# Two-branch graph convolution: shorter first turns, splits in three pieces, block additions held behind the split

## The chip, the cores and the metric

One core of one Trainium2 chip runs the whole program. The metric is the device time of one execution in microseconds; the median of the runs is compared, and a profile of one execution is at hand.

## What is computed

```python
def _gcn_layer(x, adj, W, b):
    d_inv_sqrt = (jnp.sum(adj, axis=1) + 1e-09) ** (-0.5)
    msg = d_inv_sqrt[:, None] * adj * d_inv_sqrt[None, :] @ x
    return jax.nn.relu(msg @ W + b)
H_f = _gcn_layer(feature_x, adj, W_f, b_f)
H_s = _gcn_layer(spatial_x, adj, W_s, b_s)
attn = jax.nn.sigmoid(jnp.concatenate([H_f, H_s], axis=1) @ W_att + b_att)
out = _layernorm(x + attn * H_f + (1.0 - attn) * H_s, axis=-1)
```

`adj` is 4096 x 4096 in f32, both feature matrices are 4096 x 128. The heavy part is `adj @ (d * [x, spatial_x])`, a 4096 x 4096 by 4096 x 256 product. The scale `d` of a row needs the sum over that whole row of `adj`.

## The kernel before

The contraction is cut into 32 j-tiles of 128 rows (t = 0 to 31) and the output columns into eight groups of 512 (g0 to g7). A block is one j-tile against one group; an **item** is four blocks, and there are 64 items. `plan` (L24) writes their order by hand. Blocks of one group that follow one another accumulate in PSUM as a **run**; four runs at a time form a **turn** of a set of groups, g0 to g3 or g4, g6, g5, g7, and the two sets alternate. The front (items 0 to 47) walks through j-tiles 0 to 23: the early turns take one, two or three tiles, the later ones four, where the two old tiles come first ("column" items, two tiles of two groups) and the two new tiles behind ("spread" items, one tile of four groups).

Each item passes through these queues:

- SyncE (SP) issues all loads in one fixed order: `load_item` (L333) brings the 1 MB `raw` block of item k into one of three buffers, `load_part` (L345) half a j-tile's rows of `adj` (`nat`, 1 MB) for the row sums, and `load_x` (L358) feature rows. `load_item(k)` waits until item k-3 was split and, where it was added up, until its block additions are done.
- ScalarE (ACT): `row_sum` (L696) of the parts listed under `parts[k]`, then `high` (L685), which rounds `raw` into `Ah`. After the first piece of an item it makes `Yh` of a new j-tile (`y_high`, L709), which waits for the scale `D`.
- GpSimd (POOL): for each k first `degree` (L796), which turns the two row sums of a tile into `D`, then `sum_block` (L834), which adds two of the four blocks of an item of the set g4 to g7 into `S` (these sums serve the last tiles' scales). The order on POOL is fixed: `degree`, `sum_block`, next k.
- VectorE (DVE): `low` (L489) makes `Al = raw - Ah`, `y_low` (L498) makes `Yl`, and `evacuate` (L517) moves finished runs from PSUM into `acc`.
- TensorE (PE): `block_of` (L390) issues six 128x512 matmuls per block (`Ah` with `Yh`, `Ah` with `Yl`, `Al` with `Yh`, for two halves), 24 per item. In a spread item a block's two halves follow each other, in a column item both tiles come in one half and then in the other (`sweeps`, L90).

`high` and `low` work in pieces (L305): item 0 in four, items 1 to 19 (`HALVED`) in two of 1024 columns, later items whole. For items below `HALVED` the order on DVE is: two runs of the turn that ended, first piece, `y_low`, one more run, second piece, last run (L616 to L635). A block on PE waits for the piece that holds it (L467).

The items of the front, with their j-tile (u: set g0 to g3, v: set g4 to g7, c: column item):

```
item   0   1   2   3   4   5   6   7   8   9   10    11    12  13  14    15    16  17
       0u  0v  1v  1u  2u  2v  3v  3u  4u  5u  45vc  45vc  6v  7v  67uc  67uc  8u  9u
```

Of the kernel before, what the change touches and what calls it, by code (L numbers as in the profile page):

```python
# [13 lines left out]
GT = 4  # L14
# [2 lines left out]
NATS = 3  # L17
YRING = 8
ROWS = 12
HALVED = 20  # L20
WARM = [14, 8, 3]


def plan(T):  # L24

    G = T // GT
    FRONT = T - 2 * GT
    runs, items = [], []

    def add_runs(gs, tiles, pairs):
        new = [len(runs) + i for i in range(len(gs))]  # L40
        runs.extend((g, tiles, pair, (0, IB)) for g, pair in zip(gs, pairs))
        return new

    def column(new, tiles):
        blocks = [(e, t) for e in new for t in tiles]
        items.extend(blocks[i:i + 4] for i in range(0, len(blocks), 4))

    def spread(new, tiles):
        items.extend([(e, t) for e in new] for t in tiles)

    sets = [[0, 1, 2, 3], [4, 6, 5, 7]]
    for n, tiles in enumerate([[0], [0, 1], [1, 2], [2, 3], [3, 4, 5]]):
        spread(add_runs(sets[n % 2], tiles, range(4)), tiles)
    for n in range(3, FRONT // 2):
        old, fresh = [2 * n - 2, 2 * n - 1], [2 * n, 2 * n + 1]
        new = add_runs(sets[n % 2], old + fresh, range(4))
        column(new, old)
        spread(new, fresh)
    tiles = [FRONT - 2, FRONT - 1]
    column(add_runs(sets[0], tiles, [0, 1, 2, 0]), tiles)  # L60

    first = len(runs)
    s6, s7 = list(range(FRONT, FRONT + GT)), list(range(FRONT + GT, T))
    runs.extend((g, s6 + s7, (g + 1) % 3, (0, IB)) for g in range(G - 1))
    runs.append((G - 1, s6 + s7, 2, (0, IB // 2)))
    runs.append((G - 1, s6 + s7, 0, (IB // 2, IB)))
    order = [(0, s6), (1, s6), (0, s7), (1, s7)] + [(g, s) for g in range(2, G - 1) for s in (s6, s7)]
    order += [(G - 1, s6 + s7), (G, s6 + s7)]
    items.extend([(first + g, t) for t in s] for g, s in order)
    return runs, items  # L70


def build(nc, At, adj, xs_in, W_f, W_s, b_f, b_s, W_att, b_att, out):
# [5 lines left out]
    G = T // GT  # L79
# [4 lines left out]
    FINAL = K - 2 * G  # L84
# [43 lines left out]
    PLAIN_FROM = len(SUMMED) * P  # L128
    parts = {k: [] for k in range(K)}
    parts[0], parts[2] = [0, 1], [2, 3]  # L130
    parts[4], parts[6], parts[8], parts[9] = [4, 5], [6, 7], [8, 9], [10, 11]
    for n in range(12, 30):
        parts[n - 2].append(n)
    for n in range(30, 2 * FULL):
        parts[n - 3].append(n)
# [27 lines left out]
    y_at = {k: [] for k in range(K)}  # L163
    for r in range(T):
        y_at[y_position(r)].append(r)
    X_AFTER = {y_position(m * GT) - (2 if m == 1 else 4): m for m in range(1, G)}
    assert len(X_AFTER) == G - 1

    H_F, H_S, H_ALL = slice(0, H), slice(H, H2), slice(0, H2)
    DIF = slice(H2, H2 + F)  # L170
# [26 lines left out]
    with ExitStack() as ctx:  # L197
# [6 lines left out]
        def sem(name):  # L204
            return ctx.enter_context(nc.semaphore(name))
# [40 lines left out]
        raw0_in = [sem("raw0_first"), sem("raw0_second")]  # L246
        nat1_first = sem("nat1_first")
        nat_in = [sem(f"nat_in{i}") for i in range(NATS)]
        x_early = [sem("x_first"), sem("x_second")]
        xs_sem = [sem(f"xs_in{i}") for i in range(G)]  # L250
        const_in = sem("const_in")
        pool_const = sem("pool_const")
        rs_act = sem("rs_act")
# [10 lines left out]
        low_ok = sem("low_ok")  # L264
# [40 lines left out]
        def pieces(k):  # L305

            if k == 0:
                return [(i, i + 1) for i in range(GT)]
            return [(0, 2), (2, GT)] if k < HALVED else [(0, GT)]

        def z_of(r):

# [20 lines left out]
        def _(sp):  # L333
# [24 lines left out]
            def load_x(m):  # L358
                sp.dma_start(xs[:, m * GT:(m + 1) * GT, :], xs_v[m]).then_inc(xs_sem[m], 16)

            sp.dma_start(xs[:, 0:1, :], xs_v[0, :, 0:1, :]).then_inc(x_early[0], 16)
            for k in range(K):
                for n in parts[k]:
                    load_part(n)
                if k == 2:
                    sp.dma_start(xs[:, 1:2, :], xs_v[0, :, 1:2, :]).then_inc(x_early[1], 16)
                if k == 4:
                    sp.dma_start(xs[:, 2:GT, :], xs_v[0, :, 2:GT, :]).then_inc(xs_sem[0], 16)
                load_item(k)
                if k in X_AFTER:  # L370
                    load_x(X_AFTER[k])
                if k == FINAL + 1:
                    sp.dma_start(Wfs[:, 0:H], W_f).then_inc(const_in, 16)
                    sp.dma_start(Wfs[:, H:H2], W_s).then_inc(const_in, 16)
                    sp.dma_start(bias[:, 0:H], bf_v).then_inc(const_in, 16)
                    sp.dma_start(bias[:, H:H2], bs_v).then_inc(const_in, 16)
                    sp.dma_start(watt[:, :], watt_v).then_inc(const_in, 16)
                    sp.dma_start(batt[:, :], batt_v).then_inc(const_in, 16)
# [109 lines left out]
        def _(dve):  # L488
# [124 lines left out]
            for k in range(K):  # L613
                ended = [e for e in evac_order if end_item[e] == k - 2]
                ending = [e for e in evac_order if end_item[e] == k - 1]
                if k < HALVED:  # L616
                    evacuate_new(ending[:2])
                else:
                    if len(ended) == GT:
                        evacuate_new(ended[:3])  # L620
                    if len(ending) == GT:
                        evacuate_new(ending[:1])
                for a, b in pieces(k):
                    low(k, a, b)
                    if a == 0:
                        if k >= HALVED and len(ending) == GT:
                            evacuate_new(ending[:2])
                        if k in (FINAL - 1, FINAL):
                            evacuate_new(ending[:1])
                        for r in y_at[k]:  # L630
                            y_low(r)
                        if k < HALVED:
                            evacuate_new(ending[:3])
                if k < HALVED or k in (FINAL - 1, FINAL):
                    evacuate_new(ending)  # L635
                if k == COLLECT + 2:
                    column_sums()
                mixing, joining = group_at(k, L_MIX), group_at(k, L_JOIN)
                if mixing is not None:
                    for r in of_group(mixing):  # L640
                        affine(r)
                if joining is not None:
                    for r in of_group(joining):
                        join(r)
                if mixing is not None:
                    for r in of_group(mixing):
                        logit(r)
                if k < K - 1:
                    evacuate_new(ended)
# [34 lines left out]
        def _(act):  # L684
# [23 lines left out]

            def y_high(r):  # L709
                act.wait_ge(D_ok, r + 1)  # L710
                if r < 2:
                    act.wait_ge(x_early[r], 16)
                else:
                    act.wait_ge(xs_sem[r // GT], 16)
                if r >= YRING:
# [79 lines left out]
        def _(pool):  # L795
# [36 lines left out]
                pool.tensor_tensor(D[:, a:b], dg[:, a:b], mhalf[:, 0:b - a], ALU.pow).then_inc(D_ok, b - a)  # L832

            def sum_block(k, j):  # L834
                g = runs[items[k][j][0]][0] - BY_COLUMN[0]
                n = blocks_summed(k - 1) + summed_blocks(k).index(j)
                raw_here(pool, k)
                if n >= 1:
                    pool.wait_ge(block_sum_ok, n)
                pool.tensor_tensor(S[:, g, :], S[:, g, :], raw[:, k % RAWS, j * IB:(j + 1) * IB],  # L840
# [96 lines left out]
```

## Time and profile before

| | us |
|---|---|
| median of 3 runs | 394.38 (394.3 to 394.52) |
| the profiled execution, its own time | 394.35 |
| its span, first to last instruction | 392.6 |
| PE busy in the span | 376.2 |
| DVE, ACT, POOL busy | 303.9, 283.8, 161.8 |

The span is 1.75 us shorter than the execution. Times in the rows further down are counted from the start of the span. A busy PE says only that some matmul is in its pipeline: how fast it goes is seen from the starts of consecutive matmuls.

### The profile page before, as it was taken

How to read it: one execution, taken by the hardware profiler on the slowest of the kernel's cores; microseconds unless marked ns; L12 is line 12 of the kernel's file. 1: busy time of each engine (PE TensorE's matmuls, PEld its weight loads, DVE VectorE, ACT ScalarE, POOL GpSimd, SP SyncE). 2: the span in 40 equal slices, each digit the busy share in tenths (PEclk: the TensorE clock that was granted, in tenths of full speed). 3: DMA queues.
4: the chain of work that ended last, by engine and by line, in shares of the span. 5: the costliest groups of instructions: out<-in, count | busy, mean ns of one | idle time of the engine just before them, and what ended most of it. 6: DMA issues, size and time to landing. Idle time of an engine off the chain costs nothing. (4 is left out here: it accounts for less than half of the span.)

```text
span 392.6 us, 5474 instructions
## 1 busy us (share of the span) xinstructions
PE 376.2 (96%) x1778; PEld 314.7 (80%) x1778; DVE 303.9 (77%) x434; ACT 283.8 (72%) x364; POOL 161.8 (41%) x199
## 2 busy tenths in 40 slices
PE   7779999999999999999999999999999999999990
PEld 7668778778888888888888888888788888888990
DVE  2889996979668875959589593929977887888896
ACT  3777788788878887887868887878633566668464
POOL 2343601770067603782259200010000427787764
PEclk9999999999999999999999999999999999999996
DMA  7999999999999999999999999999575434354001
GB/s 276 424 416 423 419 419 424 418 422 419 422 417 422 425 417 423 417 422 422 419 422 419 414 416 421 417 416 390 222 276 191 192 124 187 126 194 122 28 28 54
DMA packets 24508, 130.77 MB, mean 333 GB/s; under 512 B 2848, under 2 KB 7840, under 8 KB 10400
## 3 DMA queue, kind: packets, MB, share of 16 engines
q1 hardware_dynamic: 24480, 130.43, 82.6%
q8 instruction: 14, 0.23, 0.2%
q14 instruction: 14, 0.11, 0.1%
HBM read 128.32 MB, written 2.10 MB: 332 GB/s over the span
## 5 line engine op out<-in xcount | busy, mean ns | idle before, releaser
L398 PE MATMUL sums<-Ah,Yh 128*128 128x512 f32 (+1 forms) x528 | 203.7, 386 | 5.4 <-DVE Yl L503 5.0
L400 PE MATMUL sums<-Al,Yh 128*128 128x512 f32 (+1 forms) x528 | 202.1, 383 | 0.0
L399 PE MATMUL sums<-Ah,Yl 128*128 128x512 f32 (+1 forms) x528 | 202.1, 383 | 0.0
L494 DVE TENSOR_TENSOR Al<-raw,Ah 128x2048 fp32r<-128x2048 f32 (+2 forms) x86 | 159.5, 1861 | 32.2 <-ACT Ah L690 32.2
L690 ACT ACTIVATE Ah<-raw 128x2048 fp32r<-128x2048 f32 (+2 forms) x86 | 125.8, 1475 | 50.4 <-DMA raw<-in_At 31.5
L398 PEld LDWEIGHTS sums<-Ah,Yh 128*128 128x128 f32 x528 | 99.2, 188 | 27.3 <-DVE Yl L503 6.6
L400 PEld LDWEIGHTS sums<-Al,Yh 128*128 128x128 f32 x528 | 99.2, 188 | 19.6
L399 PEld LDWEIGHTS sums<-Ah,Yl 128*128 128x128 f32 x528 | 99.3, 188 | 19.0
L700 ACT ACTIVATE nat<-nat 128x2048 f32<-128x2048 f32 (+1 forms) x54 | 100.1, 1854 | 19.8 <-DMA nat<-in_adj 19.1
L514 DVE TENSOR_TENSOR acc<-sums,acc 128x512 f32<-128x512 f32 (+1 forms) x122 | 78.3, 675 | 36.6 <-PE sums L400 36.6
L840 POOL TENSOR_TENSOR S<-S,raw 128x512 f32<-128x512 f32 x40 | 69.2, 1730 | 27.5 <-DMA raw<-in_At 24.3
L798 POOL TENSOR_SCALAR dg<-rs 128x1 f32<-128x1 f32 x23 | 15.5, 672 | 106.4 <-ACT nat L700 106.2
L846 POOL TENSOR_TENSOR fin<-fin 128x128 f32<-128x128 f32 x29 | 13.9, 478 | 33.5 <-ACT fin L724 33.5
L733 ACT ACTIVATE fin<-xs,less 128x128 f32<-128x128 f32 x30 | 11.7, 390 | 17.9 <-POOL less L852 17.9
L503 DVE SCALAR_TENSOR_TENSOR Yl<-xs,D,Yh 128x256 fp32r<-128x256 f32 x32 | 22.0, 702 | 0.0
L847 POOL TENSOR_TENSOR xs<-xs,fin 128x128 f32<-128x128 f32 x29 | 20.7, 713 | 0.0
L558 DVE SCALAR_TENSOR_TENSOR xs<-fin,att,xs 128x128 f32<-128x128 f32 x30 | 12.3, 423 | 8.6 <-POOL xs L847 8.5
L717 ACT ACTIVATE Yh<-xs,D 128x256 fp32r<-128x256 f32 x32 | 15.4, 496 | 3.5 <-PE sums L400 1.8
L801 POOL TENSOR_TENSOR D<-dg,mhalf 128x1 f32<-128x1 f32 x23 | 15.8, 689 | 1.9
L408 PEld LDWEIGHTS sums<-Wfs,acc 128*128 128x128 f32 x128 | 15.6, 191 | 0.7
L408 PE MATMUL sums<-Wfs,acc 128*128 128x128 f32 x128 | 16.0, 276 | 0.0
L724 ACT ACTIVATE fin<-nat 128x256 f32<-128x256 f32 x32 | 11.4, 408 | 4.8 <-DVE nat L528 4.7
(51 smaller groups left out, 135.7 us busy)
## 6 DMA issues: line engine op xcount, KB each, us to landing
raw<-in_At SPq DMA_DIRECT2D x63, 1024.0 KB, 9.0
nat<-in_adj SPq DMA_DIRECT2D x47, 1024.0 KB, 11.6
nat<-in_adj SPq DMA_DIRECT2D x8, 768.0 KB, 9.4
xs<-in_xs SPq DMA_DIRECT2D x7, 512.0 KB, 10.4
out<-xs SPq DMA_DIRECT2D x32, 64.0 KB, 1.6
nat<-in_adj SPq DMA_DIRECT2D x2, 512.0 KB, 6.9
raw<-in_At SPq DMA_DIRECT2D x2, 512.0 KB, 8.3
xs<-in_xs SPq DMA_DIRECT2D x2, 128.0 KB, 7.0
```

The source lines that it names most:

```text
L398: pe.matmul(to, Yh[:, t % YRING, hs], high, start=first, stop=False)
L399: pe.matmul(to, Yl[:, t % YRING, hs], high, start=False, stop=False)
L400: mm = pe.matmul(to, Yh[:, t % YRING, hs], low, start=False, stop=last)
L408: return pe.matmul(sums[:, 3, bank, c + half * H:c + (half + 1) * H], acc[:, r // GT, half, q * P:(q + 1) * P], Wfs[:, half * H:(half + 1) ...
L494: dve.tensor_tensor(Al[:, k % SPLITS, a * IB:b * IB], raw[:, k % RAWS, a * IB:b * IB], Ah[:, k % SPLITS, a * IB:b * IB], ALU.subtract).the ...
L503: dve.scalar_tensor_tensor(out=Yl[:, r % YRING, :], in0=xs[:, r, :], scalar=D[:, r:r + 1], in1=Yh[:, r % YRING, :].bitcast(F32), op0=ALU.mult,
L514: dve.tensor_tensor(acc[:, g, half, a:b], sums[:, pair, half, 0:b - a], acc[:, g, half, a:b], ALU.add).then_inc(evac_ok, 1)
L690: act.activation(Ah[:, k % SPLITS, a * IB:b * IB], raw[:, k % RAWS, a * IB:b * IB], ACT.Copy).then_inc(high_ok, b - a)
L700: act.activation(nat[:, n % NATS, 0:width], nat[:, n % NATS, 0:width], ACT.Copy, accum_out=rs[:, r, h:h + 1]).then_inc(rs_act, 1)
L801: pool.tensor_tensor(D[:, r:r + 1], dg[:, r:r + 1], mhalf[:, 0:1], ALU.pow).then_inc(D_ok, 1)
L840: pool.tensor_tensor(S[:, g, :], S[:, g, :], raw[:, k % RAWS, j * IB:(j + 1) * IB], ALU.add).then_inc(block_sum_ok, 1)
L847: pool.tensor_tensor(xs[:, r, 0:F], xs[:, r, 0:F], f[:, H_S], ALU.add).then_inc(res_ok, 1)
```

## The change

The first turns are now of tiles 0; 0, 1; 1, 2; 2, 3; 3, 4; 4, 5; and 5, 6, 7, so there is one turn more, and every later turn goes to the other set. The early items up to 19 are split in three pieces (one block, one block, two blocks) on ACT and DVE, with `y_low` behind the first piece and the third run's evacuation behind the second. `sum_block` waits until all four blocks of its item are split. Five parts of the row sums (10 to 14) are due one item later, and the features of tiles 2 to 11 arrive two tiles at a time, in front of the item at which they are due; the first feature row is loaded behind the first parts.

```diff
-HALVED = 20
+STEPWISE = 20
...
-    for n, tiles in enumerate([[0], [0, 1], [1, 2], [2, 3], [3, 4, 5]]):
+    for n, tiles in enumerate([[0], [0, 1], [1, 2], [2, 3], [3, 4], [4, 5], [5, 6, 7]]):
         spread(add_runs(sets[n % 2], tiles, range(4)), tiles)
-    for n in range(3, FRONT // 2):
+    for n in range(4, FRONT // 2):
         old, fresh = [2 * n - 2, 2 * n - 1], [2 * n, 2 * n + 1]
-        new = add_runs(sets[n % 2], old + fresh, range(4))
+        new = add_runs(sets[(n + 1) % 2], old + fresh, range(4))
...
-    column(add_runs(sets[0], tiles, [0, 1, 2, 0]), tiles)
+    column(add_runs(sets[1], tiles, [0, 1, 2, 0]), tiles)
...
-    parts[4], parts[6], parts[8], parts[9] = [4, 5], [6, 7], [8, 9], [10, 11]
-    for n in range(12, 30):
+    parts[4], parts[6], parts[8], parts[10] = [4, 5], [6, 7], [8, 9], [10, 11]
+    parts[11], parts[12], parts[13] = [12], [13], [14, 15]
+    for n in range(16, 30):
         parts[n - 2].append(n)
...
-    X_AFTER = {y_position(m * GT) - (2 if m == 1 else 4): m for m in range(1, G)}
+    X_EARLY = [(0, 1), (1, 2), (2, 4), (4, 6), (6, 8), (8, 10), (10, 12)]
+    X_BEFORE = {y_position(a): i for i, (a, b) in enumerate(X_EARLY) if i >= 1}
+    X_AFTER = {y_position(m * GT) - 4: m for m in range(3, G)}
...
-            return [(0, 2), (2, GT)] if k < HALVED else [(0, GT)]
+            return [(0, 1), (1, 2), (2, GT)] if k < STEPWISE else [(0, GT)]
...
-            sp.dma_start(xs[:, 0:1, :], xs_v[0, :, 0:1, :]).then_inc(x_early[0], 16)
             for k in range(K):
                 for n in parts[k]:
                     load_part(n)
-                if k == 2:
-                    sp.dma_start(xs[:, 1:2, :], xs_v[0, :, 1:2, :]).then_inc(x_early[1], 16)
-                if k == 4:
-                    sp.dma_start(xs[:, 2:GT, :], xs_v[0, :, 2:GT, :]).then_inc(xs_sem[0], 16)
+                if k == 0:
+                    load_x_early(0)
+                if k in X_BEFORE:
+                    load_x_early(X_BEFORE[k])
                 load_item(k)
...
                         for r in y_at[k]:
                             y_low(r)
-                        if k < HALVED:
-                            evacuate_new(ending[:3])
+                    elif a == 1:
+                        evacuate_new(ending[:3])
...
                 raw_here(pool, k)
+                pool.wait_ge(low_ok, GT * (k + 1))
                 if n >= 1:
                     pool.wait_ge(block_sum_ok, n)
```

The items of the front are now:

```
item   0   1   2   3   4   5   6   7   8   9   10  11  12  13  14    15    16  17
       0u  0v  1v  1u  2u  2v  3v  3u  4u  4v  5v  5u  6u  7u  67vc  67vc  8v  9v
```

Two places of the new order matter below. The first is POOL, from the additions of item 5 on (`S`: block additions, `dg` and `D`: the two steps of `degree`, here for tiles 3, 4 and 5). Before:

```order
L840 TENSOR_TENSOR S<-S,raw 128x512 [waits block_sum_ok,raw_in2] x2
L798 TENSOR_SCALAR dg<-rs 128x1 [waits rs_act]
L801 TENSOR_TENSOR D<-dg,mhalf 128x1 [waits dg_ok]
L840 TENSOR_TENSOR S<-S,raw 128x512 [waits block_sum_ok,raw_in0] x2
L798 TENSOR_SCALAR dg<-rs 128x1 [waits rs_act]
L801 TENSOR_TENSOR D<-dg,mhalf 128x1 [waits dg_ok]
L798 TENSOR_SCALAR dg<-rs 128x1 [waits rs_act]
L801 TENSOR_TENSOR D<-dg,mhalf 128x1 [waits dg_ok]
```

Now, for the same tiles, with the additions of items 5, 6 and 9:

```order
L849 TENSOR_TENSOR S<-S,raw 128x512 [waits block_sum_ok,low_ok,raw_in2] x2
L805 TENSOR_SCALAR dg<-rs 128x1 [waits rs_act]
L808 TENSOR_TENSOR D<-dg,mhalf 128x1 [waits dg_ok]
L849 TENSOR_TENSOR S<-S,raw 128x512 [waits block_sum_ok,low_ok,raw_in0] x2
L805 TENSOR_SCALAR dg<-rs 128x1 [waits rs_act]
L808 TENSOR_TENSOR D<-dg,mhalf 128x1 [waits dg_ok]
L849 TENSOR_TENSOR S<-S,raw 128x512 [waits block_sum_ok,low_ok,raw_in0] x2
L805 TENSOR_SCALAR dg<-rs 128x1 [waits rs_act]
L808 TENSOR_TENSOR D<-dg,mhalf 128x1 [waits dg_ok]
```

The additions wait for `low_ok` as well, and those of item 9 now stand in front of tile 5's `degree`; those of item 5 stood in front of tile 3's already, without that wait.

The second place is DVE at items 14 and 15 (column items; `Yl` is that of tile 8, which item 16 is the first to use). Before:

```order
L514 TENSOR_TENSOR acc<-sums,acc 128x512 [waits evac_ok,half_done] x4
L494 TENSOR_TENSOR Al<-raw,Ah 128x1024 [waits raw_in2,high_ok,early_done]
L514 TENSOR_TENSOR acc<-sums,acc 128x512 [waits evac_ok,half_done] x2
L494 TENSOR_TENSOR Al<-raw,Ah 128x1024 [waits raw_in2,high_ok,early_done]
L514 TENSOR_TENSOR acc<-sums,acc 128x512 [waits evac_ok,half_done] x2
L494 TENSOR_TENSOR Al<-raw,Ah 128x1024 [waits raw_in0,high_ok,early_done]
L503 SCALAR_TENSOR_TENSOR Yl<-xs,D,Yh 128x256 [waits early_done,D_ok,Yh_ok]
L494 TENSOR_TENSOR Al<-raw,Ah 128x1024 [waits raw_in0,high_ok,early_done]
```

Now:

```order
L521 TENSOR_TENSOR acc<-sums,acc 128x512 [waits evac_ok,half_done] x4
L501 TENSOR_TENSOR Al<-raw,Ah 128x512 [waits high_ok,raw_in2,early_done] x2
L521 TENSOR_TENSOR acc<-sums,acc 128x512 [waits evac_ok,half_done] x2
L501 TENSOR_TENSOR Al<-raw,Ah 128x1024 [waits raw_in2,high_ok,early_done]
L521 TENSOR_TENSOR acc<-sums,acc 128x512 [waits evac_ok,half_done] x2
L501 TENSOR_TENSOR Al<-raw,Ah 128x512 [waits high_ok,raw_in0,early_done]
L510 SCALAR_TENSOR_TENSOR Yl<-xs,D,Yh 128x256 [waits early_done,D_ok,Yh_ok]
L501 TENSOR_TENSOR Al<-raw,Ah 128x512 [waits high_ok,raw_in0,early_done]
L501 TENSOR_TENSOR Al<-raw,Ah 128x1024 [waits raw_in0,high_ok,early_done]
```

In item 15 (`raw_in0`) only one block now stands in front of `Yl`, where two stood, and the turn at items 14 to 17 is now of the set that is added up on POOL.

## Rows read from the trace of the kernel before

**Rows 1.** The page, busy us of each engine, share of the span, instructions.
```profile
PE 376.2 (96%) x1778; PEld 314.7 (80%) x1778; DVE 303.9 (77%) x434; ACT 283.8 (72%) x364; POOL 161.8 (41%) x199
```
**Rows 2.** Busy time by stretch (from:to, us, engines, clock, DMA share, GB/s).
```profile
100.00:280.00 180.00, 180.00 (x804) 149.29 (x803) 131.51 (x125) 143.39 (x133) 68.20 (x60) 1.00 1.00 412
```
**Rows 3.** Waits of the whole span: total us, times, longest.
```profile
POOL dg L798 <- ACT nat L700: 106.2, 21, 10.3
...
PE sums L398 <- DVE Yl L503: 5.0, 3, 2.2
...
PEld sums L398 <- DVE Al L494: 1.4, 3, 0.6
```
**Rows 4.** Timeline of PE (start, took), 88 matmuls in step, first and last.
```profile
120.06 0.39 PE L399 MATMUL sums<-Ah,Yl 128*128 128x512 f32 x1
...
139.78 0.39 PE L399 MATMUL sums<-Ah,Yl 128*128 128x512 f32 x1
```
**Rows 5.** Timeline of PE around the first matmuls of items 2, 6, 10, 13.
```profile
23.73 0.39 PE L400 MATMUL sums<-Al,Yh 128*128 128x512 f32 x1
26.30 0.50 PE L398 MATMUL sums<-Ah,Yh 128*128 128x512 f32 x1 [2.18 <-DVE Yl L503]
26.63 0.40 PE L399 MATMUL sums<-Ah,Yl 128*128 128x512 f32 x1
...
48.25 0.39 PE L400 MATMUL sums<-Al,Yh 128*128 128x512 f32 x1
49.42 0.50 PE L398 MATMUL sums<-Ah,Yh 128*128 128x512 f32 x1 [0.78 <-DVE Yl L503]
...
71.14 0.39 PE L400 MATMUL sums<-Al,Yh 128*128 128x512 f32 x1
71.67 0.50 PE L398 MATMUL sums<-Ah,Yh 128*128 128x512 f32 x1
...
87.90 0.39 PE L400 MATMUL sums<-Al,Yh 128*128 128x512 f32 x1
88.41 0.50 PE L398 MATMUL sums<-Ah,Yh 128*128 128x512 f32 x1
```
**Rows 6.** Timeline of DVE: copies, splits of two widths, Yl alone and beside POOL.
```profile
12.45 1.90 DVE L494 TENSOR_TENSOR Al<-raw,Ah 128x512 fp32r<-128x512 f32 x3
14.26 2.48 DVE L511 COPY acc<-sums 128x512 f32<-128x512 f32 x4
...
36.61 0.48 DVE L503 SCALAR_TENSOR_TENSOR Yl<-xs,D,Yh 128x256 fp32r<-128x256 f32 x1
...
41.63 1.21 DVE L494 TENSOR_TENSOR Al<-raw,Ah 128x1024 fp32r<-128x1024 f32 x1
...
47.87 1.50 DVE L503 SCALAR_TENSOR_TENSOR Yl<-xs,D,Yh 128x256 fp32r<-128x256 f32 x1
```
**Rows 7.** Timeline of POOL: degree, and additions in pairs.
```profile
14.47 2.73 POOL L840 TENSOR_TENSOR S<-S,raw 128x512 f32<-128x512 f32 x2 [3.18 <-DMA raw<-in_At]
...
43.75 0.30 POOL L798 TENSOR_SCALAR dg<-rs 128x1 f32<-128x1 f32 x1 [3.27 <-ACT nat L700]
44.13 1.46 POOL L801 TENSOR_TENSOR D<-dg,mhalf 128x1 f32<-128x1 f32 x1
45.57 3.52 POOL L840 TENSOR_TENSOR S<-S,raw 128x512 f32<-128x512 f32 x2
...
55.35 0.56 POOL L801 TENSOR_TENSOR D<-dg,mhalf 128x1 f32<-128x1 f32 x1
```
**Rows 8.** Timeline of ACT: rounding of one and two blocks, Yh.
```profile
11.73 1.66 ACT L690 ACTIVATE Ah<-raw 128x512 fp32r<-128x512 f32 x3
...
22.32 1.06 ACT L690 ACTIVATE Ah<-raw 128x1024 fp32r<-128x1024 f32 x1 [0.87 <-DMA raw<-in_At]
...
45.63 0.51 ACT L717 ACTIVATE Yh<-xs,D 128x256 fp32r<-128x256 f32 x1 [0.36 <-POOL D L801]
```
**Rows 9.** The page, DMA issues: line, count, KB each, median us to landing.
```profile
raw<-in_At SPq DMA_DIRECT2D x63, 1024.0 KB, 9.0
```

More of the change, by code:

```diff
@@ L165, in build @@
         y_at[y_position(r)].append(r)
-    X_AFTER = {y_position(m * GT) - (2 if m == 1 else 4): m for m in range(1, G)}
-    assert len(X_AFTER) == G - 1
+    X_EARLY = [(0, 1), (1, 2), (2, 4), (4, 6), (6, 8), (8, 10), (10, 12)]
+    X_BEFORE = {y_position(a): i for i, (a, b) in enumerate(X_EARLY) if i >= 1}
+    X_AFTER = {y_position(m * GT) - 4: m for m in range(3, G)}
+    assert len(X_BEFORE) == len(X_EARLY) - 1 and len(X_AFTER) == G - 3
     H_F, H_S, H_ALL = slice(0, H), slice(H, H2), slice(0, H2)
@@ L248, in build @@
         nat_in = [sem(f"nat_in{i}") for i in range(NATS)]
-        x_early = [sem("x_first"), sem("x_second")]
-        xs_sem = [sem(f"xs_in{i}") for i in range(G)]
+        x_early = [sem(f"x_early{a}") for a, b in X_EARLY]
+        xs_sem = {m: sem(f"xs_in{m}") for m in range(3, G)}
         const_in = sem("const_in")
@@ L359, in load_x, with load_x_early @@
                 sp.dma_start(xs[:, m * GT:(m + 1) * GT, :], xs_v[m]).then_inc(xs_sem[m], 16)
-            sp.dma_start(xs[:, 0:1, :], xs_v[0, :, 0:1, :]).then_inc(x_early[0], 16)
+            def load_x_early(i):
+                a, b = X_EARLY[i]
+                c = a % GT
+                sp.dma_start(xs[:, a:b, :], xs_v[a // GT, :, c:c + b - a, :]).then_inc(x_early[i], 16)
             for k in range(K):
@@ L615, in _ @@
                 ending = [e for e in evac_order if end_item[e] == k - 1]
-                if k < HALVED:
+                if k < STEPWISE:
                     evacuate_new(ending[:2])
@@ L625, in _ @@
                     if a == 0:
-                        if k >= HALVED and len(ending) == GT:
+                        if k >= STEPWISE and len(ending) == GT:
                             evacuate_new(ending[:2])
@@ L631, in _ @@
                             y_low(r)
-                        if k < HALVED:
-                            evacuate_new(ending[:3])
-                if k < HALVED or k in (FINAL - 1, FINAL):
+                    elif a == 1:
+                        evacuate_new(ending[:3])
+                if k < STEPWISE or k in (FINAL - 1, FINAL):
                     evacuate_new(ending)
@@ L710, in y_high @@
                 act.wait_ge(D_ok, r + 1)
-                if r < 2:
-                    act.wait_ge(x_early[r], 16)
+                if r < X_EARLY[-1][1]:
+                    act.wait_ge(next(x_early[i] for i, (a, b) in enumerate(X_EARLY) if r < b), 16)
                 else:
```

## The prediction

> **What bounds it now.** I read the busy times first: PE has 376.2 of 392.6 us [rows 1]. The stretches show where that holds: from 100 to 280 us PE is busy without a gap at full granted clock, and DMA is full as well [rows 2]. PE's own pace stands in its timeline: 87 steps take 19.72 us, so a matmul starts every 0.2267 us and an item of 24 lasts 5.44 us [rows 4]. Nothing beside PE matters there unless it makes PE wait. The view of waits says where that happens: PE waits three times, 5.0 us together, for `Yl`, the low half of a new j-tile's features, and the weight loads three times for the split `Al`, 0.6 us at most [rows 3]. In the timeline these are the first matmuls of items 2, 6, 10 and 13 [rows 5]. A stall is the step from the matmul in front less 0.2267, plus 0.11, because the second step after a wait is 0.33 instead of 0.2267. That gives 2.45 us (item 2), 1.05 (6), 0.41 (10) and 0.39 (13). For items 1 and 5, which wait for the split, I take 0.5 together, an estimate from the row with 1.4 us in three waits. The sum is **4.8 us**, all ahead of 90 us: that is all the change can win in the stream. The reader should also see that POOL's `degree` waited 106.2 us in 21 waits for row sums [rows 3], so the scale `D` is made the moment its row sum is there. POOL is never late for it.
>
> **The prices.** Copies and evacuations start every 0.60 us: (2.48 - 0.68) / 3, where 0.68 is one copy [rows 6]. A 512-wide split takes 0.69 and the next starts after 0.605, (1.90 - 0.69) / 2 [rows 6]; a 1024-wide one takes 1.21 [rows 6]. Two additions on POOL take 2.73 us alone and 3.52 with a two-input DVE instruction between them [rows 7]. `dg` is 0.30, `D` 0.56 [rows 7]; with about 0.08 between, a `degree` is 0.94. From `D` to the first matmul: `Yh` 0.51 [rows 8], `Yl` 0.48 [rows 6], and 0.2 for three hand-overs, estimated at under 0.1 each from the one shown, `D` ending at 44.13 + 1.46 = 45.59 and `Yh` starting at 45.63 [rows 7, 8]: 1.19.
>
> **The step that decides: `degree` queued behind additions that now start late.** Take a turn's first item k of the set that POOL adds up (items 5 and 9, followed by a new tile). Count from the start of item k-1. The second run of the old turn leaves PE after twelve matmuls, at 2.94 (12 x 0.2267, 0.16 for the last to drain, 0.06 hand-over). DVE then does its last copy (0.60), two one-block splits (1.21), two evacuations (1.2) and the two-block split (1.21): 7.16, which is 1.72 after item k begins. Before, the additions ran when `raw` had landed; now they start here. They take 2.73 to 3.52; I take 3.1, because the next item's first split falls between them. Then `degree`, 0.94, and 1.19 to PE: 1.72 + 0.06 + 3.1 + 0.94 + 1.19 = 7.0. PE wants the tile at 5.44. The stall is 1.5, with the restart **1.6 us at item 6 and 1.6 at item 10**; by the ends 2.73 and 3.52 it is 1.3 to 2.1. Queued behind the late `D` are POOL's next additions, on ACT the rest of `high` (it stands behind `y_high`), on DVE the rest of the split, and on SP the load of item k+3.
>
> **Item 2.** Copies from 14.26 [rows 6], then the same chain: 14.26 + 2.4 + 1.21 + 1.2 + 1.21 = 20.3. Additions until 23.1. Item 2's first split (its `raw` is rounded from 22.32 [rows 8]) gets in front of `dg`, which I take as 0.4 lost: `D` is there at 23.1 + 0.4 + 0.94 = 24.4 and PE starts at 25.6. It could start at 23.6 (23.73 + 0.23 [rows 5], less 0.3 for item 1's wait, which goes). With the restart **2.2 us**. Here the one-block piece and the undisturbed `Yl` win back what the late `degree` loses. **Items 1 and 5**: the split is in time, 0. **Item 13**: its two row sums now both stand in item 13 on ACT; I leave its 0.4 as it was, between 0 and 0.8.
>
> **Item 15.** POOL's turn is now at items 14 to 17. Item 14's split ends 1.7 to 2.6 after it begins (2.6 if DVE comes late out of item 13's stall). Tile 8's `degree` is behind item 14's additions, `D` at 5.5 to 6.6. Item 15 does not need tile 8, but its second block stands behind `y_high` on ACT and `y_low` on DVE. From `D`: 0.04, 0.40 until `Yh` lets the next go, 0.63 rounding a block ((1.66 - 0.63) / 2 = 0.52 apart [rows 8]), 0.1, 0.67 split and hand-over: 1.84, so 7.3 to 8.4. As a column item it wants its second block three matmuls in, at 6.12. Stall 1.2 to 2.3, restart 0.1: I take **2.1**, nearer the upper end, because DVE does come late. Before, two blocks stood in front of `Yl` and there were no additions here.
>
> **Item 17** needs tile 9, whose `degree` is behind the additions of items 15 and 16, two pairs in a row of 2.73 to 3.52 each from the end of item 15's split, against two items of 5.44: 0 to 1.9, I take **1.2**. **Small ones**: the third piece arrives 0.2 to 0.3 late at items 3, 7, 11 and 18, where DVE started late, with the restart about 0.35 each; and at items 24 to 26 ACT, held by `y_high` of tile 12, is up to 1.2 late. That is 0 to 2.6; I take half, **1.3**.
>
> **Costed at nothing.** Four more runs are eight evacuations, 4.8 us of DVE, and the third piece adds 0.076 to each of 19 items: both lie beside PE, except as counted above. The Trainium skill, VectorE: DVE Perf Modes, section on the TRN2 errata (SBUF-src ops pay a fixed extra latency per instruction), puts an instruction at (N + 151) / 0.96 ns, so a further piece would cost 0.157 us. The durations here agree, 0.69 for 512; the starts, 0.605 apart, do not, since instructions overlap. By the page the stalls at items 6 and 10 would each be 0.08 longer. The first feature row moves behind three loads: `nat` goes out one issue earlier, but the start hangs on `raw` landing, rounding and split, so 0. Feature pairs let the `raw` behind them land earlier, which nobody waits for. Loads of items k+3 leave some 3 us later; 9.0 us lie between issue and landing in the median [rows 9], so 6 stay.
>
> **Sum.** After: 2.2 + 1.6 + 1.6 + 0.4 + 2.1 + 1.2 + 1.3 = 10.4. Before: 4.8. The difference is +5.6 on the profiled execution's 394.35, which stands 0.03 under the median of the runs: **400.0 us**. With all low ends (2.2, 1.3, 1.3, 0, 1.3, 0, 0) it is 6.1 and 395.7; with all high ends (2.2, 2.1, 2.1, 0.8, 2.4, 1.9, 2.6) 14.1 and 403.7.
>
> **Rivals.**
> - *Faster.* `Yl` took 1.50 beside an addition and 0.48 alone [rows 6]: DVE and POOL hold each other up. Additions behind the split fall beside evacuations, which go unhurt: four copies in 2.48 from 14.26 [rows 6] while POOL added from 14.47 [rows 7]. If `D` is in time, items 6, 10 and 13 lose nothing, and item 2 only 0.7 (22.32 + 0.63 + 1.2 = 24.15): 4.8 becomes 1.1, **390.7 us**. It decides if the last piece ends by 0.5 after item k begins (5.44 less 2.73, 0.94, 1.19), which would need DVE 1.2 us earlier; against it stands the run that PE frees only at 2.94. The Trainium skill, GPSIMD Engine Reference, Specifications, says the same of the port: contention comes with DVE instructions with two SBUF inputs. The trace agrees, and by that rule alone this would be the result. Chance 0.10.
> - *The late turn is harmless.* If DVE has worked ahead at items 14 to 17, only items 2, 6, 10 and 13 stall: 5.8, so 395.4; with item 6 and 10 at their low ends it is within the noise. Chance 0.15, a third of it within 0.2%.
> - *Loads starve.* If the 3 us later issue leaves DMA idle, about 1 us at four of the held loads, landings slip by 4: **404 us**. For it: DMA is full [rows 2]; against it: rows 9. Chance 0.09.
>
> **Numbers.** The forecast has 0.66, the rivals 0.15, 0.09 and 0.10. Range 395.2 to 404.0: the two ends of the sum and most of the second and third rival. 0.2%, 0.8 us, is about what a measurement of this kernel can tell from no change. Faster 0.10, same 0.05, slower 0.85.
>
> **What would show it.** In the changed profile: POOL's `dg` is released by its own queue instead of ACT, its wait for `nat` falls well under 106 us; additions in pairs of 2.73 beside evacuations; `Yl` at 0.48; PE waits for `Yl` of about 1.5 at items 6 and 10, and for `Al` inside item 15. I am wrong if `dg` still follows its row sum at once, or if PE runs through items 9 to 18 without a wait over 0.5 us.

## The result, and the profile after

The changed kernel takes **408.53 us** in the median of 5 runs (407.39 to 409.42), the kernel before 394.52 in 5 runs beside it (394.3 to 394.64): a ratio of 1.0358, 95% interval 1.0337 to 1.0379, so +14.0 us, slower. The forecast had the side and the mechanism, but less than half of the size: 400.0, with 404.0 as the upper end. The profiled execution took 409.42 (span 407.6), 15.07 over that of before. Where an execution of a kernel below was disturbed, its time is left out; for two kernels (wait late only; first feature row first, wait kept) that was the profiled one, so they are told by times alone.

The page of the changed kernel; the first line answers to [rows 1], the second is the granted TensorE clock in 40 slices, the group lines have busy us and mean ns of one, then the idle time before and what ended most of it; the last answers to [rows 9].

```profile
PE 381.8 (94%) x1778; PEld 314.9 (77%) x1778; DVE 301.6 (74%) x461; ACT 280.5 (69%) x383; POOL 146.4 (36%) x199
...
PEclk9699999999999999999999999999999999999996
...
L849 POOL TENSOR_TENSOR S<-S,raw 128x512 f32<-128x512 f32 x40 | 58.8, 1470 | 101.9 <-issue 71.6
L724 ACT ACTIVATE Yh<-xs,D 128x256 fp32r<-128x256 f32 x32 | 15.5, 500 | 47.1 <-POOL D L808 47.1
L805 POOL TENSOR_SCALAR dg<-rs 128x1 f32<-128x1 f32 x23 | 13.1, 567 | 65.5 <-ACT nat L707 64.5
...
raw<-in_At SPq DMA_DIRECT2D x63, 1024.0 KB, 7.8
```

DVE and POOL are *less* busy than before, though DVE has 27 instructions more: what they were meant to win, they won. An addition takes 1.47 us in the mean, and the feature operations are quick. But additions wait 71.6 us for something that isn't a transfer, and ACT waits 47.1 us for `D`, in 15 of 32 tiles.

The view of waits of the changed kernel (total us, times, longest), beside [rows 3]:

```profile
POOL S L849 <- issue: 71.6, 11, 11.1
POOL dg L805 <- ACT nat L707: 64.5, 13, 8.4
ACT Yh L724 <- POOL D L808: 47.1, 15, 7.4
...
POOL S L849 <- DVE Al L501: 26.9, 6, 12.3
...
PE sums L405 <- DVE Yl L510: 9.7, 6, 3.2
```

`dg` follows its row sum in 13 cases instead of 21, and that wait fell from 106.2 to 64.5: in the others `degree` stood behind additions. PE now waits 9.7 us for `Yl`, 5.0 before.

PE's timeline at items 6, 10, 15 and 17, which the forecast named, then at items 24, 25 and 35, which it did not (what stands in brackets is the idle time in front); the first group answers to [rows 5].

```profile
50.50 0.39 PE L407 MATMUL sums<-Al,Yh 128*128 128x512 f32 x1
52.27 0.50 PE L405 MATMUL sums<-Ah,Yh 128*128 128x512 f32 x1 [1.38 <-DVE Yl L510]
...
76.25 0.50 PE L405 MATMUL sums<-Ah,Yh 128*128 128x512 f32 x1 [1.38 <-DVE Yl L510]
...
106.47 0.50 PE L405 MATMUL sums<-Ah,Yh 128*128 128x512 f32 x1 [1.52 <-DVE Al L501]
...
118.00 0.50 PE L405 MATMUL sums<-Ah,Yh 128*128 128x512 f32 x1 [0.99 <-DVE Yl L510]
...
157.51 0.47 PE L405 MATMUL sums<-Ah,Yh 128*128 128x512 f32 x1 [0.63 <-DVE Al L501]
...
164.82 0.50 PE L405 MATMUL sums<-Ah,Yh 128*128 128x512 f32 x1 [1.61 <-DVE Yl L510]
...
221.35 0.50 PE L405 MATMUL sums<-Ah,Yh 128*128 128x512 f32 x1 [1.30 <-DVE Al L501]
```

By the forecast's own measure (the step less 0.2267, and the slower second step) items 2 to 18 lose 9.5 us, items from 20 on 6.9; before it was 4.8 and about 0.4. The start costs the rest. PE's first matmul in the kernel before, then the first ones in the changed kernel, and its clock from 13.2 to 16.2 us (from:to, us, engines' busy time, clock, DMA share, GB/s):

```profile
12.55 0.50 PE L398 MATMUL sums<-Ah,Yh 128*128 128x512 f32 x1 [2.03 <-DVE Yl L503]
...
13.27 0.80 PE L405 MATMUL sums<-Ah,Yh 128*128 128x512 f32 x1 [3.25 <-DVE Yl L510]
13.86 0.63 PE L406 MATMUL sums<-Ah,Yl 128*128 128x512 f32 x1
...
19.28 0.40 PE L407 MATMUL sums<-Al,Yh 128*128 128x512 f32 x1
```

```profile
13.20:16.20 3.00, 2.93 (x7) 2.35 (x8) 2.44 (x5) 1.85 (x5) 0.00 (x0) 0.50 1.02 431
```

PE was idle for 3.25 us, and then the granted clock is 0.50, that is 1.2 GHz: 14 steps take 6.01 us instead of 3.17. Before, the first matmul stood at 12.55 behind 2.03 us of idling, and the clock was 1.00 (2.4 GHz) from 12.5 to 16 us. With the start at 13.27 instead of 12.55 that is 2.73 (2.84 less the slower second step, which both have) + 0.72 = 3.45. **The ledger of the profiled executions**: 3.45 + (9.5 - 4.8) + (6.9 - 0.4) = 14.65 of 15.07. Of the 6.9, 5.3 lie in items 24 to 41; 1.6 lie at the end of the front (PE's steps at 292.65 and 296.10).

### The profile page after: what moved, and what is told of

The parts are those of the page before. It is cut to its first block and busy times, and to the rows that moved or that the text cites. A ratio compares the mean times of both kernels' runs of the same rounds, so it can differ in the third digit from the quotient of the medians.

```text
span 407.6 us, 5537 instructions
## 1 busy us (share of the span) xinstructions
PE 381.8 (94%) x1778; PEld 314.9 (77%) x1778; DVE 301.6 (74%) x461; ACT 280.5 (69%) x383; POOL 146.4 (36%) x199
## 5 line engine op out<-in xcount | busy, mean ns | idle before, releaser
L405 PE MATMUL sums<-Ah,Yh 128*128 128x512 f32 (+1 forms) x528 | 206.4, 391 | 14.8 <-DVE Yl L510 9.7
L501 DVE TENSOR_TENSOR Al<-raw,Ah 128x2048 fp32r<-128x2048 f32 (+2 forms) x105 | 157.0, 1507 | 41.9 <-ACT Ah L697 41.0
L521 DVE TENSOR_TENSOR acc<-sums,acc 128x512 f32<-128x512 f32 (+1 forms) x130 | 82.9, 675 | 19.0 <-PE sums L407 19.0
L849 POOL TENSOR_TENSOR S<-S,raw 128x512 f32<-128x512 f32 x40 | 58.8, 1470 | 101.9 <-issue 71.6
L724 ACT ACTIVATE Yh<-xs,D 128x256 fp32r<-128x256 f32 x32 | 15.5, 500 | 47.1 <-POOL D L808 47.1
L805 POOL TENSOR_SCALAR dg<-rs 128x1 f32<-128x1 f32 x23 | 13.1, 567 | 65.5 <-ACT nat L707 64.5
L510 DVE SCALAR_TENSOR_TENSOR Yl<-xs,D,Yh 128x256 fp32r<-128x256 f32 x32 | 16.5, 532 | 24.0 <-ACT Yh L724 24.0
L855 POOL TENSOR_TENSOR fin<-fin 128x128 f32<-128x128 f32 x29 | 13.9, 479 | 31.5 <-ACT fin L731 31.5
L415 PE MATMUL sums<-Wfs,acc 128*128 128x128 f32 x128 | 16.2, 277 | 0.1
L808 POOL TENSOR_TENSOR D<-dg,mhalf 128x1 f32<-128x1 f32 x23 | 12.9, 561 | 1.9
```

The lines of the kernel that those rows point to most:

```text
L405: pe.matmul(to, Yh[:, t % YRING, hs], high, start=first, stop=False)
L415: return pe.matmul(sums[:, 3, bank, c + half * H:c + (half + 1) * H], acc[:, r // GT, half, q * P:(q + 1) * P], Wfs[:, half * H:(half + 1) ...
L501: dve.tensor_tensor(Al[:, k % SPLITS, a * IB:b * IB], raw[:, k % RAWS, a * IB:b * IB], Ah[:, k % SPLITS, a * IB:b * IB], ALU.subtract).the ...
L510: dve.scalar_tensor_tensor(out=Yl[:, r % YRING, :], in0=xs[:, r, :], scalar=D[:, r:r + 1], in1=Yh[:, r % YRING, :].bitcast(F32), op0=ALU.mult,
L521: dve.tensor_tensor(acc[:, g, half, a:b], sums[:, pair, half, 0:b - a], acc[:, g, half, a:b], ALU.add).then_inc(evac_ok, 1)
L724: act.activation(Yh[:, r % YRING, :], xs[:, r, :], ACT.Copy, scale=D[:, r:r + 1]).then_inc(Yh_ok, 1)
```

## The experiments

Theory 1 was the forecast's: `degree` queues on POOL behind additions that now wait for the split. The rivals: the loads (their order at the start, or loads held by late additions), and the third piece. Each ratio is to the kernel before on the same chip, with its 95% interval.

**The one line, taken out and put in alone.** First the changed kernel without it; then the kernel before with it and nothing else.

```diff
                 raw_here(pool, k)
-                pool.wait_ge(low_ok, GT * (k + 1))
                 if n >= 1:
```

> The changed kernel without the one added wait: block additions start when their raw block has landed, all else as changed. Theory 1 (the additions, held back, hold degree and so D, Yh, Yl): the waits of PE for Yl and for the split inside items fall from about 14 us to 5 or less, additions run beside the splits again (pairs of 3.5 us), 397 to 399.5 us, of which some 3 us are the slow start. Rival (one turn more, the third piece and the other set make DVE late by themselves): less than half of the loss goes, 403 us or more.

> The kernel before with that one wait added and nothing else. Theory 1: the larger part of the loss appears with this line alone, 401 to 406 us, with POOL waiting for the split and ACT for D. Rival (turns, pieces and set): 396 us or less. The start is untouched in both: first matmul at 12.55 us.

Measured: 393.98 us without the line (0.9989, 0.9979 to 0.9998), and 410.63 with the line alone (1.0406, 1.0389 to 1.0424). The line is the whole loss; all the rest of the change together is worth 0.4 us (0.1 to 0.8 by the interval). Both went further than theory 1 expected (397 to 399.5, and 401 to 406): in particular the slow start, for which it had kept 3 us, costs nothing without the line. Without it, the waits read as before:

```profile
POOL dg L805 <- ACT nat L707: 116.6, 21, 11.3
...
POOL S L848 <- DMA raw<-in_At: 23.4, 9, 4.5
...
PE sums L405 <- DVE Yl L510: 4.6, 4, 2.8
```

**The order of the first loads.** The changed kernel with the first feature row at the head again, then the kernel before with it behind the first parts.

```diff
+            load_x_early(0)
             for k in range(K):
                 for n in parts[k]:
                     load_part(n)
-                if k == 0:
-                    load_x_early(0)
```

> The changed kernel with the first feature row loaded ahead of the first parts again. Theory 2 (the order of the first loads makes the first block land 0.7 us later and the wait before the first matmul longer, which the clock answers with its lower level for some 6 us): first matmul at 12.55, matmuls in steps of 0.227 from there, 404.5 to 406 us. Rival (the start differs from run to run, whatever the order): no change, 407.4 to 409.4.

> The kernel before with the first feature row loaded behind the first parts, nothing else. Theory 2: the first block lands near 11.4 instead of 10.6, first matmul near 13.3, the lower clock level after it, 396.5 to 398.5 us, with runs that scatter by 2 us. Rival: 394.5, no scatter.

Measured: 407.04 to 408.39 (1.0331, 1.0314 to 1.0349), about 1 us under the changed kernel, with intervals that overlap; and 394.52 (1.0001, 0.9992 to 1.001). So theory 2, that the order of the first loads costs time, falls for the kernel before. The trace of that kernel with the order turned shows why: the start was late and slow there as well, and item 2 took it up.

```profile
12.87 0.50 PE L399 MATMUL sums<-Ah,Yh 128*128 128x512 f32 x1 [2.80 <-DVE Yl L504]
...
13.87 0.63 PE L399 MATMUL sums<-Ah,Yh 128*128 128x512 f32 x1
...
26.58 0.50 PE L399 MATMUL sums<-Ah,Yh 128*128 128x512 f32 x1 [0.90 <-DVE Yl L504]
```

Item 2 waits 0.90 instead of 2.18 [rows 5] and starts 0.28 later than before. There `D` hangs on a row sum, not on PE. With the wait it hangs on the split, the split stands behind DVE's copies of item 0, and those follow PE: in the changed kernel the four copies start 1.28 apart (14.95 to 18.79), as three matmuls take 3 x 0.427. So there a slow start should go through to item 2. The kernel with the wait early only, the next experiment, bears this out: it is the same program up to item 19, its first 14 steps took 4.92 us instead of 6.01, and item 2 started at 27.45 instead of 28.30.

**The wait in one half of the items.**

```diff
-                pool.wait_ge(low_ok, GT * (k + 1))
+                if k < STEPWISE:
+                    pool.wait_ge(low_ok, GT * (k + 1))
```

> The changed kernel with the wait only in items 1 to 19, whose split goes in pieces of 512 and 1024. Theory 1 (the forecast's stalls of items 2 to 18 are right in size and what it missed lies behind item 20, each part on its own): 394.0 of the kernel without the wait, plus about 9.5 of stalls less the 2.5 that it has there, so 400 to 402. Rival (late stalls are the echo of early ones, which leave VectorE behind): this part alone gives 405 or more.

> The changed kernel with the wait only from item 20 on, whose split is one instruction of 2048. Theory 1 (what the forecast missed lies here, on its own): 394.0 plus the 6.5 of stalls that the changed kernel has behind item 20, so 399.5 to 402. Rival (late stalls are the echo of early ones): 396 or less.

Measured: early only 400.48 to 402.11 (1.0167, 1.0145 to 1.0189); late only 400.90 to 401.16 (1.0165, 1.0148 to 1.0182). Over the kernel without the wait that is 1.0167 - 0.9989 and 1.0165 - 0.9989, 7.0 and 6.9 us; together 13.9, and the whole wait costs 1.0358 - 0.9989, 14.5. The halves add up: late stalls are no echo of early ones. The stretches agree. First the changed kernel, then the one with the wait early only:

```profile
120.00:200.00 80.00, 77.74 (x340) 63.19 (x339) 58.96 (x59) 61.36 (x58) 29.33 (x28) 1.00 1.00 407
200.00:280.00 80.00, 78.21 (x351) 64.12 (x350) 49.32 (x47) 58.21 (x54) 24.31 (x26) 1.00 0.95 388
```

```profile
120.00:200.00 80.00, 79.97 (x351) 65.44 (x351) 62.07 (x60) 66.00 (x60) 36.38 (x33) 1.00 1.01 420
200.00:280.00 80.00, 80.00 (x363) 66.26 (x362) 53.83 (x52) 63.42 (x60) 18.05 (x20) 1.00 1.01 418
```

Without the late wait PE is busy almost throughout, and DMA is full again.

**Degrees ahead of the additions.** The changed kernel with the wait, POOL's order turned (and the first feature row first); the same order in the kernel before with the wait; and the first again without the wait.

```diff
-            for k in range(1, FINAL):
+            for k in range(1, FINAL + 1):
                 for r in range(1, FULL):
-                    if last_part(r) in parts[k]:
+                    if k < FINAL and last_part(r) in parts[k]:
                         degree(r)
-                for j in summed_blocks(k):
-                    sum_block(k, j)
+                for j in summed_blocks(k - 1):
+                    sum_block(k - 1, j)
```

> The changed kernel, its wait kept, but on POOL each item's degrees go ahead of the additions of the item before (and the first feature row is loaded first again). Theory 1 (the loss is D made late, since degree queues behind additions that wait for the split): D follows its row sum again, POOL's wait of dg for nat is back near 100 us, and the time is 394 to 397. Rival (the loss is the loads held up by late additions, or additions that run beside the split): additions are as late or later than in the changed kernel, so the time stays at 402 or more.

> The kernel before with the wait added and, on POOL, degrees ahead of the additions of the item before. Theory 1 (degree queued behind late additions): nearly all of the 16.1 that the wait alone cost goes, 394 to 398. Rival (held loads, or additions beside the split): 403 or more.

> The changed kernel without the wait, degrees ahead of the additions of the item before, first feature row first. With the wait this order gave 398.5, 4 more than the kernel before. Theory (those 4 are the wait's: additions behind the split hold buffers and run beside other work): 393.5 to 395. Rival (they come from the order itself, since additions now wait for a row sum): 397 or more.

Measured: 398.48 (1.0104, 1.0085 to 1.0124), 399.5 (1.0129, 1.0106 to 1.0151) and 401.66 (1.0179, 1.0164 to 1.0193). Each of the first two lies between its theory and its rival: of +14 and +16 they leave +4 and +5. With the wait kept, and the additions about as late (those of item 5 begin 2.5 us after their item, those of item 6 1.8; in the changed kernel it is 1.8 and 2.4), 10 us came back, so additions that hold their buffers long are not the main cost. POOL's `dg` waits for row sums again. The second line is one of three late steps of PE at the end of the front:

```profile
POOL dg L804 <- ACT nat L706: 126.4, 22, 12.2
...
281.07 0.50 PE L404 MATMUL sums<-Ah,Yh 128*128 128x512 f32 x1 [0.97 <-DVE acc L520]
```

The third says that the order has a cost of its own, which theory 1 had not: without any wait it is 7 us slower than before, and 3 us slower than with the wait, so in this order the wait is a gain. Part of that is the clock: behind item 2's stall it was 0.50 from 26.3 to 29.3 us there, eight steps of about 0.43, some 1.6 us, and in the first kernel it was not. By the forecast's measure the first kernel loses 5.5 us from 22 to 270 us (the changed kernel 15.0, the kernel before 4.6, the third kernel 9.2) and 2.9 behind that (1.6, 0.3 and 3.1). So most of what it still loses lies at the end of the front, where the third kernel loses it without any wait. Why, I did not follow up, and since the order moves both parts, these three do not give the share of the queue in the loss.

**The wait only without, or only with, a degree behind.** Order, pieces and loads of the changed kernel. By this rule the first run has the wait in items 2, 6, 10, 15, 17, 23, 25, 30, 32 and 38 (item 33 has a degree behind it). The second run has the condition without its "not".

```diff
-                pool.wait_ge(low_ok, GT * (k + 1))
+                if not any(last_part(r) in parts[k + 1] for r in range(1, FULL)):
+                    pool.wait_ge(low_ok, GT * (k + 1))
```

> The changed kernel with the wait only at additions that have no degree directly behind them (items 2, 6, 10, 15, 17, 23, 25, 30, 32, 33 without one in the next item as the program counts them, and 38): order, pieces and loads as in the changed kernel. Theory (only a degree queued behind late additions costs): no loss, 392.5 to 394.8; and if additions beside evacuations spare VectorE, under 394.0 of the kernel without the wait. Rival (late additions as such cost, by the buffers and loads that they hold): half of the 14 stays, 398 or more.

> The changed kernel with the wait only at additions that have a degree directly behind them, in the next item (1, 5, 9, 14, 16, 22, 24, 31, 39 and the like). Theory (a degree queued behind late additions is the whole cost): as slow as the changed kernel, 405 to 410. Rival (late additions as such): about half of the loss, 399 to 403.

Measured: 397.07 to 398.09 (1.0083, 1.007 to 1.0096) without, 411.79 to 413.25 (1.0465, 1.045 to 1.048) with a degree behind. Waits with a degree right behind cost the whole loss and more. The others cost 3.7 (1.0083 - 0.9989), a quarter, between theory and rival. Most of what the second kernel loses beyond 408.5 is seen at item 15: its additions don't wait there, so they ran beside one-block splits, and two of these took 2.89 us together (1.28 is usual).

```profile
107.75 2.89 DVE L501 TENSOR_TENSOR Al<-raw,Ah 128x512 fp32r<-128x512 f32 x2
...
109.56 0.80 PE L405 MATMUL sums<-Ah,Yh 128*128 128x512 f32 x1 [2.84 <-DVE Al L501]
110.15 0.63 PE L406 MATMUL sums<-Ah,Yl 128*128 128x512 f32 x1
```

PE waited 2.84 instead of 1.52, and then ran at 1.2 GHz until 115.6 us (clock 0.50 from 109.5 to 115.5). In the first kernel items 6 and 10 no longer wait for `Yl`, and most of what is left lies behind item 20, where a late pair still delays a degree two items on:

```profile
180.42 1.30 POOL L850 TENSOR_TENSOR S<-S,raw 128x512 f32<-128x512 f32 x1 [4.63 <-issue]
181.89 6.11 POOL L850 TENSOR_TENSOR S<-S,raw 128x512 f32<-128x512 f32 x3 [0.17 <-POOL S L850]
188.09 2.22 POOL L805 TENSOR_SCALAR dg<-rs 128x1 f32<-128x1 f32 x1
```

These are the pairs of items 30 and 31, and the `dg` is item 32's. Only item 30's pair has a wait; item 31's came late because it stood behind it, and the degree behind both.

**The third piece.** With the wait, and without it (first feature row first; the second of the two has two pieces).

```diff
-            return [(0, 1), (1, 2), (2, GT)] if k < STEPWISE else [(0, GT)]
+            return [(0, 2), (2, GT)] if k < STEPWISE else [(0, GT)]
```

> The changed kernel, wait kept, with two pieces of two j-tiles in items 1 to 19 as before. Theory (the third piece costs what the forecast has as small stalls at items 3, 7, 11 and 18, 0.35 each): 1 to 1.5 faster than the changed kernel, 406.5 to 407.7. Rival (the piece of one j-tile lets PE start earlier behind each late feature tile, so it is a gain): 409 or more.

> The changed kernel without the wait and with the first feature row loaded first again. Theory (the slow start is taken up by the wait of item 2, as where the order of loads alone was changed): 393.7 to 394.2, as without the wait. Rival (here item 2 hardly waits, 0.6, so the start counts): 392.5 to 393.4.

> The changed kernel without the wait, first feature row first, two pieces. Theory (what is left of the change, short turns and the other set, is worth a few tenths, and the third piece nothing): within 0.4 of the same kernel with three pieces. Rival (the third piece holds up VectorE): 0.5 to 1.5 faster than it, the best kernel of the study.

Measured: 409.26 with the wait (1.0377, 1.0364 to 1.0391); without it 394.24 with three pieces (1.0000, 0.9991 to 1.0009) and 394.49 with two (1.0004, 0.9996 to 1.0013). The third piece loses nothing, and with the wait it may gain up to 1 us; the intervals overlap. The first feature row's place is worth nothing here either.

**A version with the wait only where it might help**: items 2, 6, 10, 15 and 17, and the same with the first feature row first.

```diff
-                pool.wait_ge(low_ok, GT * (k + 1))
+                if k < STEPWISE and not any(last_part(r) in parts[k + 1] for r in range(1, FULL)):
+                    pool.wait_ge(low_ok, GT * (k + 1))
```

> The changed kernel with the wait only in items 2, 6, 10, 15 and 17: before item 20 and with no degree directly behind. Theory (where nothing is queued behind, additions behind the split spare VectorE, as the missing stalls at items 6 and 8 of the last run suggest): 0.5 to 1.5 under the 394.0 of the kernel without the wait, 392.5 to 393.5. Rival (a wait never gains): 394 or more.

> The same, with the first feature row loaded first again. Theory (item 2 hardly waits here, so an earlier first matmul counts): 0.3 to 1 under the same kernel with the later load. Rival (item 2 takes it up): within 0.3 of it.

Measured: 394.63 (1.0007, 0.9999 to 1.0016) and 394.5 (1.0007, 0.9997 to 1.0017). No gain: the rival holds in both. The best kernel of the study is the changed one without its wait, 0.1% under the kernel before; with the first feature row first it measured the same as the kernel before (1.0000), so this is too little to be called a gain.

## Why the forecast had the side right and the size wrong

**The deciding step was right, to a tenth, at items 6 and 10.** The timeline of POOL, DVE and ACT around item 6 in the changed kernel, beside [rows 6 to 8]:

```profile
47.13 1.29 POOL L849 TENSOR_TENSOR S<-S,raw 128x512 f32<-128x512 f32 x1 [11.11 <-issue]
48.58 1.53 POOL L849 TENSOR_TENSOR S<-S,raw 128x512 f32<-128x512 f32 x1 [0.17 <-POOL S L849]
50.21 0.30 POOL L805 TENSOR_SCALAR dg<-rs 128x1 f32<-128x1 f32 x1
50.59 0.56 POOL L808 TENSOR_TENSOR D<-dg,mhalf 128x1 f32<-128x1 f32 x1
...
45.77 1.22 DVE L501 TENSOR_TENSOR Al<-raw,Ah 128x1024 fp32r<-128x1024 f32 x1
...
51.73 0.48 DVE L510 SCALAR_TENSOR_TENSOR Yl<-xs,D,Yh 128x256 fp32r<-128x256 f32 x1 [2.76 <-ACT Yh L724]
...
51.19 0.51 ACT L724 ACTIVATE Yh<-xs,D 128x256 fp32r<-128x256 f32 x1 [3.81 <-POOL D L808]
```

Item 5 begins at 50.50 + 0.23 - 5.44 = 45.29. Its split ends at 46.99, 1.70 later (forecast 1.72); the pair of additions takes 2.98 (3.1); `degree` ends at 51.15, 1.04 behind them (0.94); PE starts at 52.27, 1.12 after that (1.19). From item 5's start it is 6.98, and 7.0 was forecast.

**Item by item.** Items 6 and 10 lose 1.65 each (1.6), item 15 1.8 (2.1), item 17 1.3 (1.2), item 13 nothing (0.4), item 2 1.4 (2.2, for a start at 25.6; it starts at 28.30, after the slow start below, which delays PE as well as the chain). The third pieces of items 3, 7, 11 and 18 and the second steps there lose 1.7. Up to item 18 the sum is 9.5, where the forecast had 9.1 and 1.3 more for small ones. That the sums agree so closely is partly luck: items 2 and 13 lose 1.2 less than forecast, and the third pieces, of which the forecast had taken half, 1.7. (Two slips in the forecast's sums are small: 25.6 less 23.6 with the restart is 2.1 for item 2, not 2.2, and the rival *Faster* has 0.7 left, not 1.1, so 390.3.)

**The step that failed: "small ones", for the turns behind item 20.** The forecast had one turn there, at items 24 to 26, with ACT "up to 1.2 late", and took half. Items from 20 on measured 6.9 in the trace (6.5 over before), and 6.9 us in the run with the wait late only. Two things were not counted. POOL has a turn there three times (items 22 to 25, 30 to 33, 38 and 39), and the chain in it is longer, since rounding and split are one instruction of 2048 each. (The 1.6 us at the end of the front are not explained by this; PE waits 0.69 of them for a copy out of PSUM.) The timeline of POOL, DVE and ACT behind item 22's split in the changed kernel:

```profile
146.45 1.28 POOL L849 TENSOR_TENSOR S<-S,raw 128x512 f32<-128x512 f32 x1 [0.17 <-POOL S L849]
147.83 2.22 POOL L805 TENSOR_SCALAR dg<-rs 128x1 f32<-128x1 f32 x1
150.14 0.56 POOL L808 TENSOR_TENSOR D<-dg,mhalf 128x1 f32<-128x1 f32 x1
...
147.16 2.72 DVE L501 TENSOR_TENSOR Al<-raw,Ah 128x2048 fp32r<-128x2048 f32 x1
...
155.07 2.29 DVE L501 TENSOR_TENSOR Al<-raw,Ah 128x2048 fp32r<-128x2048 f32 x1 [1.64 <-ACT Ah L697]
...
150.73 0.51 ACT L724 ACTIVATE Yh<-xs,D 128x256 fp32r<-128x256 f32 x1 [4.22 <-POOL D L808]
151.15 1.90 ACT L707 ACTIVATE nat<-nat 128x2048 f32<-128x2048 f32 x1
...
153.04 1.90 ACT L697 ACTIVATE Ah<-raw 128x2048 fp32r<-128x2048 f32 x1
```

The additions end at 147.73. By then the next split runs, and `dg` takes 2.22 instead of 0.30. `D` is there at 150.70. ACT stands 4.22 us before `y_high` of that tile; behind it in ACT's order are a row sum and the rounding of item 24. So item 24's split ends at 157.36, and PE, which had no need of `D` yet, starts that item at 157.51, late for `Al`. A late `D` costs through the queue of ACT, not only through the tile that needs it; the forecast had seen this at item 15 and did not carry it to the later turns.

**The start, "0".** This term failed too. It was costed at nothing because it hangs on `raw`. In the profiled execution it cost 3.45, most of it the clock at 1.2 GHz. That execution is an extreme one: in eight other traces the clock was 0.50 as well from 14.2 to 16.5 us, but 14 steps took 4.78 to 4.93 us, not 6.01. Of the eight traces with the first feature row late seven start slowly, of the eight with it first two, so a slow start goes with the new order more often but needs more than the order to explain it. The order is worth about 1 us of the time at most. That the delay went through to item 2, and wasn't taken up there, comes from the wait: 0 was right without it, as the first feature row's place shows in the kernel before (394.52 against 394.50) and in the changed kernel without the wait (1.0000 first, 0.9989 late).

**The rivals.** *Faster* had its mechanism right: `Yl` takes 0.48 at item 6 where it took 1.50 [rows 6], and an addition 1.47 in the mean where it took 1.73 (69.2 us in 40). But this frees engines that nothing waits for. *The late turn is harmless* fell (items 15 and 17 lose 3.1). *Loads starve*: DMA does dip, to a share of 0.94 from 20 to 120 us and 0.95 from 200 to 280, but ACT waited less for `raw` than before, not more. The lines of before and of the changed kernel:

```profile
ACT Ah L690 <- DMA raw<-in_At: 31.5, 48, 1.6
...
ACT Ah L697 <- DMA raw<-in_At: 19.6, 23, 2.5
```

With the degrees put ahead and the additions still late DMA is at 1.00 and 0.99 in those two stretches, and most of PE's loss is gone. So the dip looks like an effect of PE's waits rather than their cause. A kernel that holds loads alone was not tried.

**What remains open**: the 3.7 us of the waits without a degree right behind, of which the trace shows one mechanism, the delay two items on, but not that it is all of them; and why the order with degrees ahead costs 7 us by itself. That the late result goes on through ACT's queue behind item 20 is read from the traces; no run took that queue apart.

## What to carry to other kernels

Before a wait is put on an instruction, list what stands behind it on its in-order engine, and price the chain for every item in which that list has a producer that others need; one line cost 14 us here, and mostly because of the `degree` behind it: where no degree stood right behind, late additions cost a quarter. Then follow the late result one queue further: its consumer (`y_high` on ACT) also stands in an in-order queue, with work behind it that had nothing to do with it. And when a mechanism is found in early items, go through all its later turns with their own sizes before calling them small.

## What the runs showed of the hardware that was not expected

A small POOL instruction can be held for the length of a large DVE instruction, and the other way round: `dg` (128x1) took 2.22 us beside a 2048-wide split, 0.30 without one, and ended 0.17 after it; and that split, begun while an addition had 0.57 left, took 2.72 instead of 2.28. The Trainium skill, SBUF — State Buffer, section on the two separate sides, says that DVE and GpSimd share a port pair under an exclusive lock, which whichever starts first keeps for the whole instruction, where the DVE operation has two SBUF inputs and the GpSimd one reads SBUF. Both of that pair read SBUF here, and the trace agrees: `dg` is held to the end of the split, and the split takes 0.44 longer, near the 0.57 that the addition had left.

A wait of PE can cost more than its length. After 3.25 us of idling at the start and after 2.84 in the middle of the stream (item 15 of the run with a degree behind) PE was granted 1.2 GHz (clock 0.50) and lost 2.7 and 2.8 us more. The length alone doesn't tell: PE idled 2.01 at item 2 and then ran at 1.2 GHz in the kernel with degrees ahead and no wait, and in the kernel before it idled 2.18 at item 2 and stayed at 2.4 GHz (the next step is 0.33 [rows 5]). In the run with a degree behind it idled 1.83 at item 6 and again 1.83 at item 10, and fell to 1.2 GHz only behind the second (clock 0.51 from 78.0 to 81.5 us).
